# A two-layer convolution block on one core: steps of the next image enter at every second turn, and interpolation runs three pairs ahead

## The chip, the core and the metric

The kernel runs on one core of one Trainium2 chip. Its engines are TensorE (PE in the profile), VectorE (DVE), ScalarE (ACT), GpSimd (POOL) and SyncE (SP). Each takes its instructions in the order written for it, and they meet at semaphores only. The metric is the device time of one launch in microseconds (us), the median of several runs.

## What is computed

x has 8 images of 256 channels and 64x64 pixels, all in float32. Two layers follow each other, each added to its input:

```python
# layer 0: 3x3 local attention mixed with a generated 3x3 kernel
qkv = einsum('oc,bchw->bohw', w_qkv, gn(x))
attn = softmax(einsum('bhdl,bhdkl->bhkl', q, patches(k)))     # 4 heads, 9 taps
kern = einsum('hkc,bhcl->bhkl', w_kg, cat) + b_kg
x = x + w_proj @ (alpha * sum(kern * patches(v)) + beta * sum(attn * patches(v)))
# layer 1: modulated deformable 3x3 convolution of gn(x)
om = conv3x3(gn(x), w_off) + b_off          # 18 offsets, 9 masks for each pixel
v = bilinear sample of gn(x) at pixel + tap + offset, times sigmoid(mask)
x = x + einsum('bckhw,ock->bohw', v, w)
```

gn is a group normalisation over 32 groups.

## The kernel before, in words

An image is cut into 8 chunks of 512 pixels. Its work has two halves.

**The front** of an image is all of layer 0 and the preparation of layer 1. For each chunk: `xn` (ScalarE normalises x), `qkv.0` to `qkv.7` (TensorE; ScalarE evacuates each), `s` (four score steps, each two heads; after each, VectorE multiplies with a band mask, `banded`, L1303), `ext` (TensorE sums the scores to logits), `lg.out` (ScalarE), `lt` (TensorE transposes the logits), `soft.max`, `soft.exp`, `soft.mix` (VectorE and ScalarE), `soft.turn`, `soft.out` (TensorE, ScalarE), `sel` (four steps that spread the weights, each again with two band masks on VectorE), `pv` (two steps), `proj` (two steps) and `proj.end` (VectorE adds to x and takes statistics). Then `n.*` (the second normalisation), and for each chunk `pd` (ScalarE), `tp` and `om` (transposes for the table of pixels in DRAM, and the offset convolution) and `ot`, `w.pos`, `w.exp`, `w.mix` (indices and weights of the samples, mostly VectorE).

**The convolution** of an image runs over 72 units (8 chunks of 9 taps), each of two *pairs*, so m = 0 to 143. For each pair:

- `gather`: GpSimd issues two indirect DMAs (L883) that bring the four neighbours of 128 pixels each into a buffer of G (10 buffers, so 5 pairs). It waits until the interpolation five pairs before has freed it.
- `scale`: ScalarE multiplies the first neighbour by its weight (L1269). Where the offset phase of the front is running, VectorE does it (L1540).
- `lerp`: VectorE's interpolation, six operations (L1553, L1566) from G into V (6 buffers, so 3 pairs). It waits for the transposes of three pairs before.
- `turn`: TensorE first runs one contraction (`contract`, L902, four instructions of 512 columns) of an earlier unit and then transposes the pair (L1122). ScalarE copies the result to VT (L1283). After the first chunk a turn also holds `add_residual` (L1343) on VectorE, at two turns of each chunk: VectorE waits for the last contraction of the chunk before, TensorE's first contraction of the next chunk waits for that.

The convolution of image b runs together with the front of image b+1. `order_of_steps` writes one list for all engines, and every engine walks this list and picks its own parts. Generators yield the front's steps; `alternate` takes one step from each of several generators in turn, and `("idle",)` is an empty step that keeps dependent steps apart (`hop`). `fill(n, done)` takes steps until their weights (WEIGHT, at least 4 each) reach the share due at half-turn n. The banks of PSUM (six beside the two of the contraction) are handed out in the order of the list (`rotations`); TensorE waits until the last user has freed one. In the loop over m, the list before has:

```python
steps.append(("lerp", b, m))
done = fill(2 * m + 1, done)
steps.append(("turn", b, m - 1))
if m > 0:
    steps.append(("gather", b, 2 * (m - 1) + NG, 2 * m + NG))
scale(m + 2)
done = fill(2 * m + 2, done)
```

`s`, `ext`, `sel`, `pv` and `om` use a part of the TensorE array at a time (tiles of 64x128, 128x32, 32x128, 128x64); all other steps use it whole, 128x128. The first image's front runs before any convolution. The last image (`late`) has no front beside it: its convolution runs with the offset steps of its own chunks, and at every second pair ScalarE and VectorE work in halves that TensorE adds (`in_halves`, L1118, L1119, L1558).

Of the kernel before, what the change touches and what calls it, by code (L numbers as in the profile page):

```python
# [18 lines left out]
NCH = L // CH  # L19
# [5 lines left out]
NG = 10  # L25
# [6 lines left out]
PAIRS = 2 * UNITS  # L32
# [5 lines left out]
PROJ = 2  # L38
ADD = 2
HOP = 3  # L40
NEXT = 1
CHAIN = 5
COLLECT, TURN = 3, 2
NFIRST, NCONST = 9, 8
NST, ST = 6, 4
LATE_LEAD, LATE_PACE = 110, 440


# [36 lines left out]
    return late(b, NB) and m % 2 == 1  # L85


def offsets_fill(b, c, NB):


    return c + NCH if late(b, NB) else c


def alternate(*streams):
    streams = list(streams)
    while streams:
        for g in list(streams):
            step = next(g, "end")
            if step == "end":
                streams.remove(g)  # L100
            else:
                yield step


def together(*steps):
# [5 lines left out]
    return [t for s in steps for t in (s[1] if s[0] == "together" else (s,))]  # L111


def order_of_steps(NB):

    IDLE = ("idle",)
    have_kv, have_logits, have_x1 = set(), set(), set()
    offsets_run = [False]  # L120

    def hop(n):
        for _ in range(n):
            yield IDLE

    def norm(j, b):

# [25 lines left out]
    def scores(b, c):  # L153
        for par in (ODD, EVEN):
            while par == EVEN and c + 1 < NCH and (b, c + 1) not in have_kv:
                yield IDLE
            if b == 0:
                yield together(*(("s", b, c, par, hp) for hp in range(2)))
            else:
                for hp in range(2):  # L160
                    yield ("s", b, c, par, hp)
        yield from hop(COLLECT)
        yield ("ext", b, c)
        have_logits.add((b, c))
        yield ("lg.out", b, c)
        yield from hop(TURN)
        yield ("lt", b, c)

    def soften(b, c):


        if c == 0:
            yield from hop(CHAIN)
        for kind in ("soft.max", "soft.exp", "soft.mix", "soft.turn", "soft.out"):
            yield (kind, b, c)
            yield from hop(CHAIN if kind == "soft.mix" and c in (0, NCH - 2) else HOP if kind == "soft.mix" and c == NCH - 1 else 0)

    def last_scores(b, c):

# [4 lines left out]
    def mix(b, c):  # L184
        alone = 0 if c < NCH - 1 else HOP if b == 0 else NEXT
        if c < NCH - 1:
            yield from soften(b, c)
        else:
            yield from hop(2)
        while c > 0 and (b, c - 1) not in have_x1:  # L190
            yield IDLE
        for hp in range(2):

            while hp == 1 and c + 1 < NCH and (b, c + 1) not in have_logits:
                yield IDLE
            if b == 0:
                yield together(*(("sel", b, c, of, hp) for of in (OWN, BORDER)))
                continue
            for of in (OWN, BORDER):
                yield ("sel", b, c, of, hp)  # L200

                yield from hop(NEXT if c == NCH - 1 else 0)
        if b == 0:
            yield from hop(2 + alone)
            yield together(*(("pv", b, c, hp) for hp in range(2)))
            return
        for hp in range(2):
            yield from hop(1 + alone)
            yield ("pv", b, c, hp)

    def project(b, c):
        for _ in range(PROJ):
            yield IDLE
        for oh in range(2):
            yield ("proj", b, c, oh)
            for _ in range(ADD - 1):
                yield IDLE
        have_x1.add((b, c))
        yield ("proj.end", b, c)
# [59 lines left out]
            yield ("load_x", b + 1, c - 1)  # L279

    def weights(b, c):
        yield IDLE
        yield ("ot", b, c)
        yield ("w.pos", b, c)
        yield ("w.exp", b, c)
        yield ("w.mix", b, c)
# [9 lines left out]
    def offset_phase(b):  # L296

        before = iter(())
        yield ("pd", b, 0)
        yield from hop(HOP if b == 0 else NEXT)  # L300
        if late(b, NB):
            yield from table_phase(b)
            yield from offsets(b, 0)
            yield from weights(b, 0)
            return
        for c in range(NCH):
            yield from alternate(offsets(b, c), before)
            before = weights(b, c)
        yield from alternate(before, first_scores(b + 1) if b + 1 < NB else iter(()))
# [9 lines left out]
    def front(b):  # L319
        offsets_run[0] = False  # L320
        yield from layer0(b)
        offsets_run[0] = True
        yield from offset_phase(b)
        offsets_run[0] = False

    steps = list(begin())
# [2 lines left out]

    sets = (have_kv, have_logits, have_x1)  # L330
    before = [set(v) for v in sets]
    total = sum(weigh(s) for s in front(1))
    for v, old in zip(sets, before):
        v.clear()
        v.update(old)
    for b in range(NB):
        fr = front(b + 1) if b + 1 < NB else late_offsets(b)
        lead, pace = (LEAD, total) if b + 1 < NB else (LATE_LEAD, LATE_PACE)
        done = 0

        def fill(n, done):
            step = 0
            while done < lead + n * pace // (4 * UNITS) and step < BURST * pace // (4 * UNITS):
                s = next(fr, None)
                if s is None:
                    break
                steps.append(s)
                step += weigh(s)
                done += weigh(s)
            return done  # L350

        def scale(m):
            if m < PAIRS:
                steps.append(("scale", b, m, not offsets_run[0]))

        steps.append(("gather", b, 0, NG))
        scale(0)
        scale(1)
        done = fill(0, done)
        for m in range(PAIRS):  # L360
            steps.append(("lerp", b, m))
            done = fill(2 * m + 1, done)
            steps.append(("turn", b, m - 1))
            if m > 0:
                steps.append(("gather", b, 2 * (m - 1) + NG, 2 * m + NG))
            scale(m + 2)
            done = fill(2 * m + 2, done)
        steps.append(("turn", b, PAIRS - 1))
        steps.append(("conv.end", b))
        steps.extend(fr)  # L370
    return singly(steps)


# [153 lines left out]
def build(nc, x, wqk, wv, wn, wkx, bkg, alpha, beta, wproj, woff, boff, wconv,  # L527
          ident, g8, selx, selp, band, selo, base, out):
    NB = x.shape[0]
    steps = order_of_steps(NB)  # L530
# [3 lines left out]
    with ctx:  # L534
# [752 lines left out]
        def _(e):  # L1287
# [57 lines left out]
            for s in steps:  # L1345
# [222 lines left out]
                elif kind == "turn" and s[2] >= 0:  # L1568
                    b, m = s[1:]
                    u, pair = divmod(m, 2)  # L1570
                    c, t = unit(u)
                    if t == 1 and pair == 0 and u > 8:
                        add_residual(b * NCH + c - 1, 0)
                    elif t == 1 and pair == 1 and u > 8:
                        add_residual(b * NCH + c - 1, 1)
                elif kind == "conv.end":
                    for oh in range(2):
                        add_residual((s[1] + 1) * NCH - 1, oh)
# [73 lines left out]
```

## Time and profile before

| | us |
|---|---|
| median of 3 runs (5186.94 to 5206.48) | 5197.19 |
| the profiled execution | 5200.59 |
| its span | 5198.8 |
| PE busy | 4855.1 (93%) |
| DVE busy | 4324.4 (83%) |
| ACT busy | 2332.2 (45%) |
| POOL busy | 2257.9 (43%) |

The mean granted TensorE clock was 0.983 of full speed. The span goes from the first instruction to the last. A busy time counts every moment in which an engine has an instruction at work; idle time before an instruction is put down to what released it. Matmuls are pipelined, so a group's start to the next group's start says more of its cost than its length.

### The profile page before, as it was taken

To read this page: it belongs to the slowest core of one execution; us is meant where nothing else is said; L and a number is where in the kernel's file an instruction comes from. 1 tells how busy PE (TensorE), PEld (TensorE's weight loads), DVE (VectorE), ACT (ScalarE), POOL (GpSimd) and SP (SyncE) were. 2 spreads that over 40 slices of the span, in tenths; PEclk is the share of its full clock that TensorE was granted. 3 is DMA by queue.
4 is the path that set the end of the run, shared out by engine and by line. 5 is a ranking of instruction groups with operands and counts; after the bars stand their busy time and mean duration, and the time that the engine had idled before them with its cause. 6 is when DMAs were issued, how large, how long until landed. Compare 5 with 4: busy or idle time off the path is not lost. (4 is left out here: it accounts for less than half of the span.)

```text
span 5198.8 us, 80271 instructions
## 1 busy us (share of the span) xinstructions
PE 4855.1 (93%) x26864; PEld 2671.2 (51%) x26864; DVE 4324.4 (83%) x11040; ACT 2332.2 (45%) x5584; POOL 2257.9 (43%) x2311
## 2 busy tenths in 40 slices
PE   7889999999999999999999999999999999988888
PEld 4545554555545555455545555455554555544444
DVE  6848888888888888888889888888888888987776
ACT  2244444344453444444444444434444344455555
POOL 0014444444444444444444444444444444455565
PEclk9999999999999999999999999999999999999999
DMA  5447878878787878978789787888878878798888
GB/s 180 143 153 263 284 260 321 284 270 278 274 325 269 275 272 281 339 252 282 266 274 339 261 278 266 288 315 270 281 267 310 290 263 275 258 356 313 328 324 305
DMA packets 490804, 1446.79 MB, mean 278 GB/s; under 512 B 47380, under 2 KB 117404, under 8 KB 490140
## 3 DMA queue, kind: packets, MB, share of 16 engines
q0 software_dynamic: 331776, 1208.11, 66.9%
q1 hardware_dynamic: 158620, 233.55, 12.6%
q8 instruction: 219, 3.59, 0.3%
q14 instruction: 189, 1.55, 0.1%
HBM read 1309.08 MB, written 132.39 MB: 277 GB/s over the span
## 5 line engine op out<-in xcount | busy, mean ns | idle before, releaser
L883 POOL DMA_INDIRECT G<-table,IDX x2304 | 2257.0, 980 | 2902.3 <-DVE V L1566 2094.9
L902 PE MATMUL ps<-VT,s_wconv 128*128 128x512 f32 x4608 | 2273.9, 617 | 102.0 <-ACT VT L1283 37.7
L1566 DVE SCALAR_TENSOR_TENSOR V<-G,WT,V 128x256 f32<-128x256 f32 x4320 | 1892.7, 479 | 115.8 <-DVE V L1566 3.7
L1283 ACT ACTIVATE VT<-ps 128x512 f32<-128x512 f32 x1152 | 686.7, 596 | 2294.5 <-PE ps L1122 1848.3
L902 PEld LDWEIGHTS ps<-VT,s_wconv 128*128 128x128 f32 x4608 | 823.7, 193 | 919.1 <-issue 847.0
L1553 DVE SCALAR_TENSOR_TENSOR V<-G,WT 128x256 f32<-128x256 f32 x2304 | 1009.0, 478 | 244.6 <-ACT G L1269 135.4
L1122 PEld LDWEIGHTS ps<-s_ident,V 128*128 128x128 f32 x4320 | 539.1, 142 | 650.4 <-issue 647.1
L1303 DVE TENSOR_TENSOR E<-ps,s_band 128x512 f32<-128x512 f32 x1024 | 648.7, 682 | 268.9 <-PE ps L964 137.3
L1269 ACT ACTIVATE G<-G,WT 128x256 f32<-128x256 f32 x1872 | 846.4, 498 | 16.1 <-DMA G<-table,IDX 12.3
L1122 PE MATMUL ps<-s_ident,V 128*128 128x128 f32 x4320 | 655.5, 275 | 47.6 <-DVE V L1566 43.0
L940 PE MATMUL ps<-XN,s_wqk 128*128 128x512 f32 x1024 | 488.5, 605 | 19.7 <-ACT XN L1182 16.7
L964 PE MATMUL ps<-QB,KP 64*128 64x256 f32 (+2 forms) x2944 | 298.8, 340 | 2.0 <-DVE E L1303 1.3
L943 PE MATMUL ps<-s_wv,XN 128*128 128x292 f32 x1024 | 293.9, 416 | 0.0
L964 PEld LDWEIGHTS ps<-QB,KP 64*128 64x128 f32 x2944 | 235.8, 188 | 80.2 <-issue 62.6
L940 PEld LDWEIGHTS ps<-XN,s_wqk 128*128 128x128 f32 x1024 | 179.7, 191 | 183.5 <-issue 158.2
L1032 PE MATMUL ps<-E,VP 128*64 128x64 f32 (+2 forms) x3008 | 248.6, 318 | 8.2 <-DVE E L1303 8.2
L1080 PE MATMUL ps<-KP,s_woff 128*32 128x512 f32 x2048 | 244.2, 600 | 0.3 <-issue 0.3
L1045 PE MATMUL ps<-ACX,s_wproj 128*128 128x512 f32 x512 | 243.0, 598 | 1.4 <-ACT ACX L1139 1.4
L943 PEld LDWEIGHTS ps<-s_wv,XN 128*128 128x128 f32 x1024 | 180.0, 190 | 57.5 <-issue 20.1
L1032 PEld LDWEIGHTS ps<-E,VP 128*64 128x64 f32 x3008 | 171.8, 140 | 69.3 <-issue 21.1
L1233 ACT ACTIVATE KP<-X,gn 128x64 f32<-128x64 f32 (+1 forms) x396 | 192.8, 576 | 0.0
L1139 ACT ACTIVATE ACX<-ps 128x168 f32<-128x168 f32 (+1 forms) x384 | 112.3, 402 | 164.9 <-PE ps L1032 131.8
(109 smaller groups left out, 3008.4 us busy)
## 6 DMA issues: line engine op xcount, KB each, us to landing
table<-E SPq DMA_DIRECT2D x256, 256.0 KB
G<-table,IDX POOLq DMA_INDIRECT x2304
X<-in_x SPq DMA_DIRECT2D x64, 512.0 KB
G<-in_x SPq DMA_DIRECT2D x56, 512.0 KB, 4.3
x<-X SPq DMA_DIRECT2D x56, 512.0 KB, 5.5
R<-x SPq DMA_DIRECT2D x56, 512.0 KB
out<-R SPq DMA_DIRECT2D x56, 512.0 KB
out<-X SPq DMA_DIRECT2D x8, 512.0 KB
```

Of the source, the lines that this page charges most:

```text
L883: e.indirect_dma_start(G[a % NG][:, :], None, T[b % 2], bass.IndirectOffsetOnAxis(ap=IDX[:, col:col + 1], axis=0)).then_inc(d_g[a % NG], 16)
L902: mm = e.matmul(CV[oh][:, :], s_wconv[:, h, t, oh * P:(oh + 1) * P], VT[U % 2][:, h, :], start=(t == 0 and h == 0), stop=(t == 8 and h == 1))
L940: mm = e.matmul(bank[:, :], s_wqk[:, h, n * P:(n + 1) * P], XN[:, h, :], start=(h == 0), stop=(h == 1))
L943: mm = e.matmul(bank[:, 0:C + 36], XN[:, h, (n - 4) * P:(n - 3) * P], s_wv[:, h, :], start=(h == 0), stop=(h == 1))
L964: mm = e.matmul(to, k_view(g + t // 4)[part, hp, P * (t % 4):P * (t % 4) + P], QB[g % 2][part, hp, W * lo:W * hi], start=True, stop=True)
L1032: mm = e.matmul(BK[banks.place[use]][64 * (h % 2):64 * (h % 2) + 64, W * lo:W * hi], VP[:, (4 * g + t) % NVT, 64 * h:64 * h + 64], E[prods ...
L1122: mm = e.transpose(to, upper, s_ident[:, :])
L1269: e.activation(G[a % NG][:, 0:C], G[a % NG][:, 0:C], ACT.Copy, scale=WT[:, col, 0:1]).then_inc(act_scale, 1)
L1283: e.activation(VT[U % 2][:, :, 2 * P * pair:2 * P * (pair + 1)], BK[banks.place[use]][:, :].rearrange("p (h n) -> p h n", h=2), ACT.Copy). ...
L1303: e.tensor_tensor(two_rows(E[prods.place[use[0], use[1], use[3]]][:, :], *to), two_rows(BK[banks.place[use]][:, :], 0, 4, 2), band, ALU.mu ...
L1553: e.scalar_tensor_tensor(vt[:, :], gt[:, C:2 * C], WT[:, col, 1:2], gt[:, 0:C], ALU.mult, ALU.add).then_inc(lerp[0], 1)
L1566: e.scalar_tensor_tensor(vt[:, :], gt[:, q * C:(q + 1) * C], WT[:, col, q:q + 1], vt[:, :], ALU.mult, ALU.add).then_inc(lerp[q - 1], 1)
```

## The change

Three things are done to the list of steps. The convolution's own steps are reordered: `lerp` of pair m+2 and `scale` of pair m+4 stand around `turn` of pair m (before, `lerp` m+1 and `scale` m+3 did). The front's steps enter at odd m only, two fills together. And inside a front a dependent step waits for a gap (the stretch between two such entries) with `HELD` steps that don't count as progress, at most two steps with band masks enter in one gap, and in each entry `whole_first` moves `lt` and `qkv` ahead of tiled steps. `add_residual` moves with its contraction. Fronts written before `spread[0]` is set (the first image's) keep their `hop`s.

```diff
+GAP = 28
+def opened(m):
+    return m % 2 == 1
+IDLE, HELD = ("idle",), ("held",)
 def alternate(*streams):
     streams = list(streams)
     while streams:
+        moved = False
         for g in list(streams):
             step = next(g, "end")
             if step == "end":
                 streams.remove(g)
-            else:
+            elif step != HELD:
+                moved = True
                 yield step
+        if streams and not moved:
+            yield HELD
+def whole_first(part):
+    TILED, WHOLE = ("s", "ext", "sel", "pv", "om"), ("n.mean", "n.var", "qkv", "lt", "soft.turn", "proj", "tp", "ot")
+    part = list(part)
+    for i, s in enumerate(part):
+        if s[0] == "lt" or (s[0] == "qkv" and s[3] > 0):
+            to = i
+            for k in range(i - 1, -1, -1):
+                if part[k][0] in TILED:
+                    to = k
+                elif part[k][0] in WHOLE:
+                    break
+            if to < i and any(t[0] in TILED for t in part[i + 1:]):
+                part.insert(to, part.pop(i))
+    return part
...
+    def apart(n, first):
+        if not spread[0]:
+            yield from hop(first)
+            return
+        until = gaps[0] + n
+        while gaps[0] < until:
+            yield HELD
+    masked = [0, 0]
+    def masks(*step):
+        while spread[0] and masked[0] == gaps[0] and masked[1] == 2:
+            yield HELD
+        masked[:] = (gaps[0], masked[1] + 1 if masked[0] == gaps[0] else 1)
+        yield step
...
-                    yield ("s", b, c, par, hp)
-        yield from hop(COLLECT)
+                    yield from masks("s", b, c, par, hp)
+        yield from apart(1, COLLECT)
         yield ("ext", b, c)
         have_logits.add((b, c))
         yield ("lg.out", b, c)
-        yield from hop(TURN)
+        yield from apart(1, TURN)
         yield ("lt", b, c)
...
             yield (kind, b, c)
-            yield from hop(CHAIN if kind == "soft.mix" and c in (0, NCH - 2) else HOP if kind == "soft.mix" and c == NCH - 1 else 0)
+            if kind in ("soft.mix", "soft.out"):
+                yield from apart(1, 0 if kind == "soft.out" else CHAIN if c in (0, NCH - 2) else HOP if c == NCH - 1 else 0)
...
-                yield ("sel", b, c, of, hp)
-
-                yield from hop(NEXT if c == NCH - 1 else 0)
+                yield from masks("sel", b, c, of, hp)
...
+        yield from apart(1, 1 + alone)
         for hp in range(2):
-            yield from hop(1 + alone)
             yield ("pv", b, c, hp)
     def project(b, c):
-        for _ in range(PROJ):
-            yield IDLE
+        yield from apart(1, PROJ)
...
     def weights(b, c):
-        yield IDLE
+        yield from apart(1, 1)
...
         yield ("pd", b, 0)
-        yield from hop(HOP if b == 0 else NEXT)
+        yield from apart(1, HOP if b == 0 else NEXT)
...
-    total = sum(weigh(s) for s in front(1))
+    spread[0] = True
+    total = 0
+    for s in front(1):
+        total += weigh(s)
+        gaps[0] = total // GAP
...
                 if s is None:
                     break
-                steps.append(s)
+                if s == HELD and len(part) > 0 and part[-1] == HELD:
+                    break
+                part.append(s)
                 step += weigh(s)
                 done += weigh(s)
+            steps.extend(whole_first(part))
...
         done = fill(0, done)
+        interpolate(0)
+        scale(2)
+        interpolate(1)
+        scale(3)
         for m in range(PAIRS):
-            steps.append(("lerp", b, m))
-            done = fill(2 * m + 1, done)
-            steps.append(("turn", b, m - 1))
-            if m > 0:
-                steps.append(("gather", b, 2 * (m - 1) + NG, 2 * m + NG))
-            scale(m + 2)
-            done = fill(2 * m + 2, done)
-        steps.append(("turn", b, PAIRS - 1))
+            interpolate(m + 2)
+            if opened(m):
+                done = fill(2 * m + 1, done)
+                done = fill(2 * m + 2, done)
+                gaps[0] += 1
+            steps.append(("turn", b, m))
+            steps.append(("gather", b, 2 * m + NG, 2 * m + 2 + NG))
+            scale(m + 4)
         steps.append(("conv.end", b))
-        steps.extend(fr)
+        for s in fr:
+            gaps[0] += s == HELD
+            steps.append(s)
...
-                    if t == 1 and pair == 0 and u > 8:
+                    if t == 0 and pair == 1 and u > 8:
                         add_residual(b * NCH + c - 1, 0)
-                    elif t == 1 and pair == 1 and u > 8:
+                    elif t == 1 and pair == 0 and u > 8:
                         add_residual(b * NCH + c - 1, 1)
```

## Rows read from the trace of the kernel before

**Rows 1.** The page, part 1: the span, busy time and share of each engine.

```profile
span 5198.8 us, 80271 instructions
PE 4855.1 (93%) x26864; PEld 2671.2 (51%) x26864; DVE 4324.4 (83%) x11040; ACT 2332.2 (45%) x5584; POOL 2257.9 (43%) x2311
```

**Rows 2.** Windows by convolution: length, engine busy (count), granted clock, DMA share, GB/s.

```profile
2271.26:2895.73 624.47, 596.89 (x3320) 326.56 (x3318) 539.79 (x1391) 274.88 (x662) 281.27 (x289) 0.99 0.82 284
...
4155.94:4742.82 586.88, 538.84 (x2841) 292.08 (x2840) 498.00 (x1188) 284.24 (x670) 284.15 (x291) 0.98 0.83 291
4742.82:5198.80 455.98, 391.24 (x1654) 212.66 (x1652) 319.25 (x836) 258.50 (x587) 264.67 (x266) 0.94 0.87 317
```

**Rows 3.** Waits of PE in 2271.26 to 2895.73: who, total us, times, longest.

```profile
PE ps L1122 <- DVE V L1566: 5.1, 8, 1.9
PE ps L902 <- DVE R L1343: 4.8, 2, 2.5
PE ps L989 <- ACT LS L1139: 4.6, 2, 3.1
PE ps L1013 <- DVE E L1303: 2.8, 2, 1.5
PE ps L1013 <- ACT ACX L1134: 2.5, 1, 2.5
PE ps L940 <- ACT XN L1182: 2.2, 3, 1.2
```

**Rows 4.** PE's timeline, 2000 to 2020: start, length, line, count, [idle before].

```profile
2001.29 0.60 PE L1122 MATMUL ps<-s_ident,V 128*128 128x128 f32 x4
2001.73 1.88 PE L902 MATMUL ps<-VT,s_wconv 128*128 128x512 f32 x4
2003.61 0.63 PE L1122 MATMUL ps<-s_ident,V 128*128 128x128 f32 x4
2004.17 2.42 PE L979 MATMUL ps<-E,s_selx 128*32 128x176 f32 x48
2006.53 1.98 PE L902 MATMUL ps<-VT,s_wconv 128*128 128x512 f32 x4
...
2011.71 0.41 PE L1013 MATMUL ps<-ACX,s_selp 32*128 32x176 bf16 x6 [2.54 <-ACT ACX L1134]
2012.05 3.67 PE L902 MATMUL ps<-VT,s_wconv 128*128 128x512 f32 x4
```

**Rows 5.** A short window at that wait, columns as in Rows 2.

```profile
2010.70:2014.10 3.40, 2.39 (x9) 1.21 (x10) 3.21 (x8) 0.95 (x5) 2.50 (x3) 0.70 0.99 391
```

**Rows 6.** PE's timeline, 2234 to 2246, a wait and the group behind it.

```profile
2237.83 1.95 PE L979 MATMUL ps<-E,s_selx 128*32 128x176 f32 x48 [1.46 <-DVE E L1303]
2239.71 1.99 PE L902 MATMUL ps<-VT,s_wconv 128*128 128x512 f32 x4
```

**Rows 7.** The page's groups of VectorE's masks and of ScalarE's normalisation.

```profile
L1303 DVE TENSOR_TENSOR E<-ps,s_band 128x512 f32<-128x512 f32 x1024 | 648.7, 682 | 268.9 <-PE ps L964 137.3 <-PE ps L1013 70.3 <-issue 35.0
...
L1182 ACT ACTIVATE XN<-X,gn 128x512 f32<-128x512 f32 x114 | 85.7, 801 | 0.5 <-DVE gn L1404 0.5
```

**Rows 8.** DVE's timeline, 2267 to 2280, at the start of a convolution.

```profile
2269.48 0.30 DVE L1424 TENSOR_REDUCE sm<-ps 128x16 f32<-128x144 f32 x1
...
2271.23 0.87 DVE L1553 SCALAR_TENSOR_TENSOR V<-G,WT 128x256 f32<-128x256 f32 x2
2272.02 1.85 DVE L1566 SCALAR_TENSOR_TENSOR V<-G,WT,V 128x256 f32<-128x256 f32 x4
2273.79 0.30 DVE L1432 TENSOR_REDUCE sm<-SC 128x16 f32<-128x144 f32 x1
...
2276.42 0.87 DVE L1553 SCALAR_TENSOR_TENSOR V<-G,WT 128x256 f32<-128x256 f32 x2
```

**Rows 9.** Waits of PE, then of ACT, in the last convolution, 4742.82 to 5198.80.

```profile
PE ps L902 <- ACT VT L1283: 36.7, 8, 7.3
...
ACT VT L1283 <- remote: 99.7, 29, 6.6
```

More of the change, by code:

```diff
@@ L111, in singly @@
     return [t for s in steps for t in (s[1] if s[0] == "together" else (s,))]
+def whole_first(part):
[12 more added lines that the diff above has]
+    return part
 def order_of_steps(NB):
-    IDLE = ("idle",)
     have_kv, have_logits, have_x1 = set(), set(), set()
     offsets_run = [False]
+    gaps = [0]
+    spread = [False]
     def hop(n):
@@ L342, in fill @@
             step = 0
+            part = []
             while done < lead + n * pace // (4 * UNITS) and step < BURST * pace // (4 * UNITS):
@@ L354, in scale, with interpolate @@
                 steps.append(("scale", b, m, not offsets_run[0]))
+        def interpolate(m):
+            if m < PAIRS:
+                steps.append(("lerp", b, m))
         steps.append(("gather", b, 0, NG))
```

## Prediction, written before the changed kernel ran

> **What bounds the kernel now.** I read the page's busy shares first, then windows by convolution, then the waits of TensorE, then its timeline. TensorE is busy 4855 of 5199 us, VectorE 4324, ScalarE and GpSimd under half [rows 1]. A convolution with the next image's front beside it takes 624.5 us; TensorE is busy 596.9 of it, VectorE 539.8, and the DMA share is 0.82 [rows 2]. So TensorE sets the time, and what can be won there is its idle time, 624.47 - 596.89 = 27.6 us an image (4.4%), and what hides inside its busy time. The waits say what the idle time is: transposes that wait for the interpolation (5.1 us), contractions that wait for the residual (4.8), and front steps that wait for a step of their own chain on VectorE or ScalarE (4.6 for `lt`, 2.8 and 2.5 for `sel`, 2.2 for `qkv.0`) [rows 3]; the six make 22.0, and the remaining 5.6 are smaller ones of the same kinds.
>
> Two costs lie inside the busy time. The first is the change between the whole array and a tiled step. From the start of four transposes to the next contraction it is 2001.73 - 2001.29 = 0.44 us, to a tiled step 2004.17 - 2003.61 = 0.56; a contraction group takes 1.88 behind whole work and 1.98 behind tiled work [rows 4]. That is 0.12 + 0.10 = 0.22 us for each block of tiled steps. The second is the clock: behind the wait of 2.54 us the contraction took 3.67 us instead of 1.88 [rows 4], and the granted clock in that stretch was 0.70 [rows 5], so part of it ran at 1.2 GHz and not at 2.4. Behind a wait of 1.46 us the next contraction took 1.99 [rows 6]: no loss.
>
> By the Trainium skill (TensorE: Matmul & The Clock Gate, "A second HAM failure mode: psum-queue depth-cycling") frequent short idles between groups of matmuls alone can make the clock swing to half. Rows 6 speak against that here; what the rule would give is rival 2's price in every gap.
>
> **The change, part by part.** All is per image, of the six convolutions with a full front; a gap is two pairs, 624.5 / 72 = 8.7 us.
>
> (a) Switches. In the list before, the 112 tiled steps of an image (32 s, 32 sel, 8 ext, 16 pv, 24 om) stand in 91 blocks: a turn or a `qkv` is between most of them. After, they enter at 72 places instead of some 288, s and sel come in twos, both pv together, and `qkv` and `lt` are moved out from between them. I count 8 blocks for ext, 15 for s, 14 for sel, 8 for pv and some 9 for om: 54. 37 fewer at 0.22 is **-8 us** (bounds: 70 blocks, -5; 45, -10).
>
> (b) Waits that a gap removes. `ext` comes a gap after the masks, `lt` after the logits' copy, `sel` after `soft.out`, `pv` after its masks, `soft.turn` after `soft.mix`, `proj` after `pv`, `tp` after the first `pd`. A gap of 8.7 us covers what they wait for: ScalarE's copies, and masks of 4 x 0.68 = 2.7 us behind one interpolation [rows 7, 8]. So 4.6 + 2.8 + 2.5 and about 3 of the small ones go: **-13**.
>
> (c) The residual. TensorE's contraction for t = 0 comes two turns after the last contraction of the chunk before. VectorE's additions now stand at the same turns as those last contractions, one turn earlier than before. VectorE then waits where it would wait for a V buffer anyway. 4.8 goes: **-5**.
>
> (d) Interpolation three pairs ahead of its turn, not two. In mid-image this takes the last of the 5.1 us away, but those waits lie mostly at the start of an image, where VectorE works without a break: between 2269.5 and 2276.4 it does soft.max (1.75 us), a pair (2.56) and soft.mix (2.63) back to back [rows 8]. There the run-ahead has to be built up, before the first turn: VectorE does pairs 0 to 2 ahead of turn 0, and turn 0 comes right behind the first fill, not three fills later. I set **+3** (bounds: 0, since the last pair of the image before is also one earlier; one and a half pairs, +4). The same number of gathers and scales stand the same two pairs ahead of their interpolation, with the same 10 buffers of G, so GpSimd's queue sees nothing new; SP's steps keep their order among themselves.
>
> (e) Waits that the bunching adds. What isn't held back a gap now has no turn between its links: `xn` and `qkv.0`, `n.aggr` to `n.var`. TensorE begins the fill right after turn m-1. ScalarE has a copy and a scale first and then xn, 2 x 0.80 us [rows 7]. A wait of up to 2 us in each of 7 chunks, halved because it is often covered by steps ahead of it in the fill: +7 in place of 2.2, **+5**; the norm chain **+2** (bounds together: 0 and +16). Banks: two mask steps hold four of the six, but the turn's contraction, 1.9 us, stands before the transpose that needs one. Nothing. VectorE's own lateness costs nothing as long as TensorE has two pairs in hand: in a gap it needs 2 x 2.6 us for pairs and on average (539.8 - 72 x 2 x 2.6) / 72 = 2.3 for the rest, 7.5 of 8.7 [rows 2, 8].
>
> (f) Clock. Waits of over 2 us are two to three an image now [rows 3], each followed by a loss like 3.67 - 1.88 = 1.8 [rows 4]. One or two of them go: **-3** (bounds 0 and -5).
>
> Sum: -8 -13 -5 +3 +7 -3 = -19, of which -8 is idle time: 27.6 falls to about 20. I take **-20**.
>
> The seventh convolution (586.9 us, with the last image's shorter front) has 48 us idle [rows 2], part of it where VectorE alone sets the pace; I set -12. The last (456.0 us) has no front: 64.7 us idle, of which 36.7 are contractions that wait for ScalarE's copy, and ScalarE itself stood 99.7 us before such copies for a source the profile doesn't name [rows 2, 9]. Interpolating earlier doesn't help a late ScalarE; it shields the pairs behind it. I set -6 (bounds 0 and -20). What comes before the first contraction is planned without gaps and stay.
>
> 6 x -20 - 12 - 6 = -138. The profiled execution took 5200.6 us, 3.4 over the median of the runs; 5200.6 - 138 = 5062.6, against the median 5059. **Prediction 5058 us.**
>
> **The rivals.**
>
> 1. *The waits only move.* Bunching gives back all that the gaps win (the +16 of (e), +4 of (d), no clock gain) and the switches remain. Per image -5 -13 -5 +4 +16 = -3, at best -6: 5197 less 18 to 36 and at most 12 of the last two, 5150 to 5180. For it: TensorE starts each fill when VectorE has just been released by the same turn. Against: most links are held a gap apart.
>
> 2. *Slower: VectorE starves the turns.* V holds three pairs, so interpolation m+2 can't start before turn m-1 has been transposed, exactly when TensorE enters the fill. In a heavy gap VectorE has soft.max and soft.mix (1.75 + 2.63), four masks (2.7), `proj.end` (four operations of 512 columns, an estimate of 2.7 by the masks' 0.68) [rows 7, 8]: 9.8 us, and two pairs, 5.2: 15.0 against 8.7. It falls 6.3 us behind, against some 8 us in hand (two turns of 2.3 and a fill). It decides where two heavy gaps follow each other, or TensorE's wait grows past 2 us: then 3 us and the clock's 1.8 for each of 8 chunks, 38 an image against the 29 that (a), (b), (c) and (f) win: 9 an image, 5197 + 6 x 9 = 5250. For it: 4324 us of VectorE is not far below. Against: the mean gap needs 7.5.
>
> 3. *The plan doesn't fit.* A chunk's chain needs about 5.3 gaps by my count (masks four to a gap's two, soft, sel, pv), its steps by weight 6.6 gaps, and 72 are there. Should holds leave steps over, they run behind the convolution, with TensorE's work the same but each wait bare: 2.5 us as the longest ones now and the clock's 1.8 [rows 3, 4], 4.3 a gap; 4 gaps left give back 17 of the 20: 5160 to 5200.
>
> **How the numbers follow.** My forecast's own cases run from 4975 (the good bounds of (a), (d), (e), (f) make -33 an image, which with -20 and -20 for the last two is 4959; all at once is unlikely) to 5150 (only -7 an image). Chance 0.68. Rival 1: 0.14, of which 0.10 lies below 5171; rival 3: 0.05; rival 2: 0.13. The range 4975 to 5190 leaves out rival 2 and a little below. A measurement of this kernel can tell about 0.5%, 26 us, from no change: faster means below 5171, slower above 5223. Faster 0.78, same 0.09, slower 0.13.
>
> **What would show it.** An image's convolution of about 604 us with TensorE idle about 20; no waits of L902 for L1343, of L989 for L1139, of L979 for L1303; more of L940 for L1182; fewer groups of 1.98 us in the timeline; one low stretch of the clock fewer. The forecast is wrong if the wait of L1122 for L1566 grows past 10 us an image, if the image takes over 620 us, or if it falls below 593.

## The result and the profile after

The changed kernel takes 5292.46 us (5275.03 to 5294.59, 4 runs), the kernel before, measured beside it, 5193.37: a ratio of 1.018, 95% interval 1.015 to 1.021. The forecast was 5058, at best 4975 and at worst 5190; it went the other way. The profiled execution is the fastest of the four, 17 us under their median, which matters for the last convolution below.

The page's first part of the changed kernel, against [rows 1]:

```profile
span 5273.2 us, 80271 instructions
PE 4820.6 (91%) x26864; PEld 2709.8 (51%) x26864; DVE 4336.0 (82%) x11052; ACT 2346.9 (45%) x5572; POOL 2253.1 (43%) x2311
```

TensorE is busy 34.5 us less and the span is 74.4 us longer, so its idle time grew by 109 us. The granted clock fell from 0.983 to 0.975. The windows run from the last transposes of one convolution to the last transposes of the next, of the changed kernel and then of the one before:

```profile
2282.26:2917.25 634.99, 591.18 (x3320) 330.99 (x3319) 541.84 (x1393) 277.08 (x658) 279.77 (x288) 0.98 0.80 280
...
4200.79:4808.15 607.36, 540.47 (x2825) 303.58 (x2823) 504.83 (x1200) 284.97 (x669) 281.63 (x287) 0.96 0.80 280
4808.15:5263.93 455.78, 404.57 (x1778) 219.50 (x1777) 333.80 (x877) 277.21 (x624) 279.76 (x280) 0.97 0.91 335
```

```profile
2250.59:2875.06 624.47, 596.90 (x3321) 326.57 (x3319) 539.73 (x1391) 274.87 (x660) 281.27 (x288) 0.99 0.82 284
...
4125.10:4715.52 590.42, 541.71 (x2825) 296.11 (x2823) 503.44 (x1200) 282.62 (x669) 282.92 (x288) 0.98 0.83 290
4715.52:5189.53 474.01, 410.64 (x1778) 221.52 (x1777) 334.94 (x877) 274.68 (x624) 277.15 (x278) 0.94 0.87 319
```

A convolution beside a full front is 10.5 us longer here (the five that can be compared lost 10.5 to 16.8), though TensorE is busy 5.7 us less in it: its idle time went from 27.6 to 43.8. The one beside the last front lost 17 us. The last one, beside no front, is 18 us shorter in this pair of executions, but that can't be put down to the change. In two more profiles of the changed kernel (under the experiments) it took 479.5 and 474.9 us, and in one more of the kernel before 471.9, so the 18 us didn't come back. The losses of the others came back: 637 to 642 us beside a full front, 612 and 613 beside the last.

What TensorE waits for in that convolution of the changed kernel, and below it what VectorE waits for in the same stretch (who, total us, times, longest):

```profile
PE ps L1191 <- DVE E L1372: 6.6, 5, 2.1
PE ps L1069 <- DVE CB L1521: 5.8, 3, 2.5
PE ps L1009 <- ACT XN L1251: 5.6, 4, 2.3
PE ps L1082 <- DVE E L1372: 4.5, 5, 1.8
PE ps L1048 <- DVE E L1372: 4.0, 2, 2.0
PE ps L987 <- DVE mv L1447: 3.9, 1, 3.9
PE ps L1191 <- DVE V L1635: 2.1, 1, 2.1
PE ps L971 <- DVE R L1412: 2.1, 2, 1.2
```

```profile
DVE V L1622 <- PE ps L1191: 47.7, 13, 12.9
DVE R L1412 <- PE ps L971: 11.8, 3, 6.9
```

The lines moved by 67 to 69: L1191 are the transposes, L1009 `qkv`, L1048 `ext`, L1082 `sel`, L1372 the masks, L1622 the first operation of an interpolation. The waits for the residual and the logits' copy [rows 3] have gone or shrunk. In their place stand waits for VectorE's masks (L1372) and small sums (CB, mv). Two of the three rows for masks are waits for a bank: transposes and `sel` read nothing that a mask writes, they need a PSUM bank that a mask has still to read. Only `ext` waits for the masks' result. And VectorE, for whose work TensorE waits, has itself stood still 47.7 us ahead of interpolations until transposes freed a buffer of V; in the same stretch of the kernel before it was 1.5 us.

How the two go together shows in timelines, TensorE's and then VectorE's (start, length, line):

```profile
2442.31 0.41 PE L1082 MATMUL ps<-ACX,s_selp 32*128 32x176 bf16 x6
2443.05 1.20 PE L1033 MATMUL ps<-QB,KP 64*128 64x192 f32 x12 [0.34 <-DVE E L1372]
2444.18 1.98 PE L971 MATMUL ps<-VT,s_wconv 128*128 128x512 f32 x4
2446.00 0.60 PE L1191 MATMUL ps<-s_ident,V 128*128 128x128 f32 x4
2446.44 1.88 PE L971 MATMUL ps<-VT,s_wconv 128*128 128x512 f32 x4
2448.16 0.60 PE L1191 MATMUL ps<-s_ident,V 128*128 128x128 f32 x4
2450.76 1.95 PE L1048 MATMUL ps<-E,s_selx 128*32 128x176 f32 x48 [2.00 <-DVE E L1372]
```

```profile
2419.74 0.88 DVE L1622 SCALAR_TENSOR_TENSOR V<-G,WT 128x256 f32<-128x256 f32 x2 [4.29 <-PE ps L1191]
...
2428.01 0.88 DVE L1622 SCALAR_TENSOR_TENSOR V<-G,WT 128x256 f32<-128x256 f32 x2 [2.27 <-issue]
...
2440.43 2.47 DVE L1372 TENSOR_TENSOR E<-ps,s_band 128x512 f32<-128x512 f32 x4
2442.83 0.87 DVE L1622 SCALAR_TENSOR_TENSOR V<-G,WT 128x256 f32<-128x256 f32 x2
2443.62 1.85 DVE L1635 SCALAR_TENSOR_TENSOR V<-G,WT,V 128x256 f32<-128x256 f32 x4
2445.56 0.88 DVE L1622 SCALAR_TENSOR_TENSOR V<-G,WT 128x256 f32<-128x256 f32 x2
2446.36 1.86 DVE L1635 SCALAR_TENSOR_TENSOR V<-G,WT,V 128x256 f32<-128x256 f32 x4
2448.14 2.48 DVE L1372 TENSOR_TENSOR E<-ps,s_band 128x512 f32<-128x512 f32 x4
```

TensorE enters at 2442.31 and again at 2448.7: this gap is 6.4 us long, not 8.7, because an entry is filled by weights and this one holds one `sel`, one `s` and twelve idle steps. For VectorE the same gap is two pairs and four masks, 2442.83 to 2450.6, 7.8 us. The masks of the first entry, whose inputs TensorE computes from 2442.31 to 2444.2, are begun at 2448.1 behind both pairs, and `ext` waits 2.0 us. The two pairs could have waited in part: the first is transposed at 2448.16, the second only at 2455.03. And VectorE has no slack left here because it stood still before: 4.29 us at 2419.74 until the transposes freed a buffer of V, and 2.27 us at 2428.01, where the profile names no source but the transposes of three pairs before end at 2427.97. From there to 2450.6 it works without a break. That the time lost there is what the masks lack here is my reading of one place; the experiments test it.

### The profile page after: what moved, and what is told of

Read it like the earlier page. It is cut to its first block and busy times, and to the rows that moved or that the text cites. A ratio compares the mean times of both kernels' runs of the same rounds, so it can differ in the third digit from the quotient of the medians.

```text
span 5273.2 us, 80271 instructions
## 1 busy us (share of the span) xinstructions
PE 4820.6 (91%) x26864; PEld 2709.8 (51%) x26864; DVE 4336.0 (82%) x11052; ACT 2346.9 (45%) x5572; POOL 2253.1 (43%) x2311
## 5 line engine op out<-in xcount | busy, mean ns | idle before, releaser
L971 PE MATMUL ps<-VT,s_wconv 128*128 128x512 f32 x4608 | 2247.6, 611 | 77.6 <-issue 38.9
L1622 DVE SCALAR_TENSOR_TENSOR V<-G,WT 128x256 f32<-128x256 f32 x2304 | 1009.6, 479 | 506.5 <-PE ps L1191 348.0
L971 PEld LDWEIGHTS ps<-VT,s_wconv 128*128 128x128 f32 x4608 | 812.1, 194 | 780.5 <-issue 709.1
L1191 PEld LDWEIGHTS ps<-s_ident,V 128*128 128x128 f32 x4320 | 540.9, 142 | 667.3 <-issue 579.0
L1191 PE MATMUL ps<-s_ident,V 128*128 128x128 f32 x4320 | 656.3, 275 | 72.3 <-DVE E L1372 49.7
L1372 DVE TENSOR_TENSOR E<-ps,s_band 128x512 f32<-128x512 f32 x1024 | 639.2, 680 | 81.1 <-PE ps L1033 53.9
L1009 PE MATMUL ps<-XN,s_wqk 128*128 128x512 f32 x1024 | 488.9, 615 | 58.7 <-ACT XN L1251 39.4
L1009 PEld LDWEIGHTS ps<-XN,s_wqk 128*128 128x128 f32 x1024 | 190.9, 196 | 277.6 <-issue 209.1
L1012 PE MATMUL ps<-s_wv,XN 128*128 128x292 f32 x1024 | 277.1, 412 | 0.0
L1101 PEld LDWEIGHTS ps<-E,VP 128*64 128x64 f32 x3008 | 187.7, 142 | 60.2 <-issue 15.1
```

Of the source, the lines that this page charges most:

```text
L971: mm = e.matmul(CV[oh][:, :], s_wconv[:, h, t, oh * P:(oh + 1) * P], VT[U % 2][:, h, :], start=(t == 0 and h == 0), stop=(t == 8 and h == 1))
L1009: mm = e.matmul(bank[:, :], s_wqk[:, h, n * P:(n + 1) * P], XN[:, h, :], start=(h == 0), stop=(h == 1))
L1012: mm = e.matmul(bank[:, 0:C + 36], XN[:, h, (n - 4) * P:(n - 3) * P], s_wv[:, h, :], start=(h == 0), stop=(h == 1))
L1101: mm = e.matmul(BK[banks.place[use]][64 * (h % 2):64 * (h % 2) + 64, W * lo:W * hi], VP[:, (4 * g + t) % NVT, 64 * h:64 * h + 64], E[prods ...
L1191: mm = e.transpose(to, upper, s_ident[:, :])
L1372: e.tensor_tensor(two_rows(E[prods.place[use[0], use[1], use[3]]][:, :], *to), two_rows(BK[banks.place[use]][:, :], 0, 4, 2), band, ALU.mu ...
```

## The experiments

The runs fell on two kinds of chip. The kernel before took 5193 to 5220 us (the slower) or 5064 to 5065 (the faster), so ratios are compared within one kind only. All ratios are to the kernel before, measured beside the variant on the same chip, with 95% intervals. The changed kernel itself ran on the slower kind only. Times of single convolutions below are from the end of one's last contraction to the end of the next one's.

**The ruler**, both kernels unchanged, on the slower chip.

> The changed kernel, unchanged, beside the same kernel before as the experiments. By theory A it is above both variants that take VectorE's wait out of the fill's way (1.005 of before each): 1.015 to 1.025. If it is at 1.005 too, theory A is wrong and the difference to the variants was the chip's.

> The changed kernel once more, so that it stands on one chip with its variants: the kernel before took 5065 us in one call and 5193 to 5220 in the two others, so ratios are to be compared within a call. Ratio 1.015 to 1.025 whichever chip this is. Both theories say the same of it; it is the ruler.

Measured 1.0166 (1.0132 to 1.0201) and 1.016 (1.0138 to 1.0183).

> The kernel before, unchanged, for a profile on the chip of the other runs of this call. If this chip is the one of the last runs (before at 5065 and not 5193), its trace says where 128 us between two chips lie: either in waits for gathers (theory of slow transfers: scales on ScalarE that wait for a gather, and the last convolution) or in TensorE's granted clock.

Its profile came from the slower chip again (span 5201.9), so it didn't tell the two chips apart. A later pair did: the same kernel (residual alone, below) ran on both. These are waits of ScalarE there, on the faster and then on the slower:

```profile
ACT G L1269 <- DMA G<-table,IDX: 65.3, 122, 1.8
```

```profile
ACT VT L1283 <- issue: 172.3, 100, 5.5
ACT VT L1283 <- remote: 130.6, 39, 7.8
...
ACT LS L1139 <- remote: 55.2, 10, 6.4
ACT ACX L1139 <- remote: 42.9, 12, 5.9
```

On the slower chip ScalarE stands up to 7.8 us before its copies for a source that the profile doesn't name; on the faster one it has no such wait. A scale stands ahead of such a copy and waits for its gather, so late gathers are my reading; it is argued, not shown. The last convolution, where nothing runs beside it, shows the same difference plainest, faster and then slower (columns as in [rows 2]):

```profile
4650.00:5047.40 397.40, 389.56 (x1776) 210.57 (x1773) 336.11 (x878) 276.69 (x614) 279.26 (x278) 1.00 0.97 379
```

```profile
4757.00:5236.40 479.40, 414.43 (x1776) 221.91 (x1774) 334.92 (x877) 269.96 (x614) 276.91 (x278) 0.93 0.86 314
```

The same instructions take 82 us longer, of 189 in the whole run; TensorE is idle 65.0 us instead of 7.8 and its granted clock is 0.93 instead of 1.00. Every profile has 397 to 408 us here on the faster kind and 456 to 487 on the slower, whatever the variant.

**The order on VectorE alone.**

```diff
-            interpolate(m + 2)
             if opened(m):
                 ...
                 gaps[0] += 1
+            interpolate(m + 2)
```

> The changed kernel with one move: at odd m the fill stands ahead of interpolation m+2 and not behind it. TensorE's and ScalarE's lists stay the same; only VectorE's order differs. Theory A (interpolating three pairs ahead fills all three pairs of V, so VectorE waits for the transposes of turn m-1 and then does a pair before it comes to the fill's masks and sums, and TensorE meets them late): the 47.7 us an image in which VectorE waits for L1191 no longer delay the fill, TensorE's waits for masks, the CB copies and mv (29 us an image in the changed kernel) fall to under 12, the time to 5130 to 5190. Theory B (entering two fills at once is what hurts, whoever stands first on VectorE): within 20 us of the changed kernel's 5290.

> The fill ahead of interpolation m+2, once more. Theory A (VectorE held up in a full V ahead of the fill's masks): at least 0.8% below the changed kernel of this call. Theory C (the gain of this variant was the chip's, whose gathers land sooner): within 0.3% of it.

Faster chip: 1.0055 (1.0038 to 1.0072). Slower, beside the ruler: 1.0039 (1.0026 to 1.0051), that is 1.2% under the changed kernel. Theory A had the size too large (5130 to 5190, or 0.988 to 0.999 of before), but its sign and its 0.8% hold, and theory C is out. TensorE's list was the same, step for step, so three quarters of the loss came from where the fill stands on VectorE. The waits of TensorE on the slower chip, over the whole run, changed kernel and this one:

```profile
PE ps L1191 <- DVE E L1372: 49.1, 37, 4.2
...
PE ps L1048 <- DVE E L1372: 43.3, 22, 2.4
...
PE ps L1082 <- DVE E L1372: 26.3, 26, 2.0
```

```profile
PE ps L1191 <- DVE E L1372: 24.4, 28, 1.3
...
PE ps L1048 <- DVE E L1372: 15.1, 8, 2.4
PE ps L1082 <- DVE E L1372: 14.4, 15, 2.0
```

118.7 us for masks became 53.9. The waits for CB (44.0 and 42.4) and mv (27.7 and 25.4) stayed, against the expectation. VectorE still waits 222.6 us for V (343.7 in the changed kernel), but at odd m it now does so behind the fill's work and not ahead of it.

**Two pairs ahead.** `interpolate(m + 1)` and `scale(m + 3)` around turn m, the rest as changed.

> The changed kernel with interpolation two pairs ahead of its turn as before (interpolation m+1 and scale m+3 around turn m); the entries at every second turn, the holds and whole_first stay. Theory A: V no longer fills up, VectorE's waits for the transposes mostly go, 5150 to 5220. Theory B: 5280 or above, since less of the run-ahead is left to cover a heavy entry; waits of the transposes for V would grow past 10 us an image.

> Interpolation two pairs ahead, once more. Theory A: at least 0.8% below the changed kernel of this call. Theory C: within 0.3% of it. Where it stands to the kernel before says what the rest of the change (entries at every second turn, holds, whole_first, residual) is worth: I expect 1.000 to 1.008.

Faster: 1.005 (1.0033 to 1.0067). Slower: 0.9989 (0.9974 to 1.0004), 1.7% under the changed kernel. The run-ahead is the whole loss there; the rest of the change, against the kernel before, is worth nothing that can be measured on the slower kind and costs 0.5% on the faster. Theory B's fear, transposes that wait for V, came to 45.5 us in all, not 10 an image.

So the forecast gain is missing here too, and the waits of TensorE over the whole run say why, kernel before and this one on the slower kind. The gap took away what it was meant to: `lt` for its logits 33.3 to 9.1, `sel` for ScalarE 17.8 to 0, the residual 35.4 to 0. But `soft.turn` now waits 43.2 us for `soft.mix` (CB; 2.0 before) though a gap lies between them, `qkv.0` 37.4 for `xn` (16.7), the norm chain 33.7 for mv and gnt (3.5), and transposes 32.4 for a bank that a mask holds (0). That is 77 us gone and 124 new.

**Three pairs ahead in the kernel before.** `lerp` m+1 ahead of turn m-1, `scale(m + 3)`.

> The kernel before with the run-ahead alone: interpolation m+1 ahead of turn m-1, scale one pair earlier, nothing else. Theory A: it is slower by itself, 5230 to 5290, with VectorE waiting for transposes (L1122) by tens of us an image, and more waits of TensorE for the masks. Theory B: run-ahead does no harm, 5170 to 5195, and the last convolution gains the 18 us that it gained in the changed kernel.

Faster: 1.0168 (1.0151 to 1.0185). The same 1.7%, without holds or double entries. VectorE waited 310.8 us for transposes (10.4 in the kernel before), and TensorE 68.8 us for the residual instead of 35.4 and 45.4 for the masks of `ext` instead of 25.1 (the profile of before is from the slower kind). The last convolution gained nothing: 406.3 us, beside 397.4 for the residual alone.

**Two pairs ahead with a V of four buffers**, so that V is as full as six are at three.

```diff
-NV = 6
+NV = 4
-                    if M > 2:
-                        e.wait_ge(*filled(("vt", M - 3)))
+                    if M > 1:
+                        e.wait_ge(*filled(("vt", M - 2)))
```

> The variant two pairs ahead with four V buffers and not six, so that two pairs ahead fill V just as three pairs ahead fill six. Theory A (a full V holds VectorE before the fill's masks): it loses what three pairs ahead lost, 1.010 to 1.020 of before, with VectorE's waits for the transposes (33.7 us in the variant with six) at 250 to 400 us. If something else of the run-ahead costs the time (the ramp at the start of an image, scales or gathers at other places), it stays within 0.3% of the variant with six, 0.996 to 1.003.

Faster: 1.0214 (1.0197 to 1.0231), against 1.005 with six. VectorE's wait for a free V, with six and with four buffers:

```profile
DVE V L1620 <- PE ps L1189: 34.7, 10, 6.0
```

```profile
DVE V L1620 <- PE ps L1189: 373.8, 120, 12.9
```

The loss came back with the full V and with nothing else of three pairs ahead. That is theory A. Transposes didn't starve (56.0 us of waits for V with six buffers, 56.3 with four); TensorE's waits for masks and their banks rose from 59.0 to 88.5. V with eight buffers at three pairs ahead, the converse, wasn't tried.

**Double entries.** First every turn, three pairs ahead:

> The changed kernel with steps entering at every turn (the two fills of each m), the gap still counted at odd m, the rest as in the change. Theory A: still slower than before, since interpolation m+2 stands ahead of each fill: 5230 to 5300. Theory B: at or below 5200, though the blocks of tiled steps rise again and with them some 8 us an image.

Faster: 1.0333 (1.0316 to 1.035), more than theory A had (5300 is 1.021 of before). Entries at every turn with two pairs ahead stand at 1.007 on the same kind of chip (without `whole_first`, below), so run-ahead costs 2.6% here instead of 1.7. My reading is that with a full V an interpolation now stands in the way of every entry, not of every second. Then the kernel before with both fills at odd m only, its hops kept:

> The kernel before with nothing but the entries at every second turn (both fills at odd m, ahead of turn m-1); hops, run-ahead and residual as before. If entering in pairs is what hurts (theory B): 1.01 or more, with TensorE's waits for the masks and XN doubled. By theory A alone: 0.995 to 1.005, blocks of tiled steps some 20 an image fewer.

Slower: 1.0695 (1.0661 to 1.0729); TensorE waited 88.5 us for the masks of `ext` and 80.1 for those of `pv`. Theory A missed (0.995 to 1.005), B has it: without holds the double entry costs 7%. A hop is counted in steps, and two fills in one entry can swallow it; that this is the reason isn't tested. (Its fills precede turn m-1 and not turn m, so it isn't the change's entry to the letter.) Then holds without double entries, two pairs ahead:

```diff
             interpolate(m + 1)
-            if opened(m):
-                done = fill(2 * m + 1, done)
-                done = fill(2 * m + 2, done)
-                gaps[0] += 1
+            done = fill(2 * m + 1, done)
+            done = fill(2 * m + 2, done)
+            gaps[0] += opened(m)
             steps.append(("turn", b, m))
```

> Entries at every turn and two pairs ahead as before, so of the change the holds of a gap, the two-mask limit, whole_first and the place of the residual are left. If entering at every second turn is a loss by itself (as the kernel before with that alone, 1.07), this is faster than two ahead: 0.985 to 1.0. If holds need the double entries (a link of the chain then stands right at a gap's edge), it is slower: 1.01 to 1.02.

> Holds, whole_first and the residual with entries at every turn, two pairs ahead, once more. If what it wins is on the slower chip only (where before loses time to late gathers in front of ScalarE's copies), 1.005 to 1.010 where before takes 5065 and 0.994 where it takes some 5215. If it is the order itself, 0.994 on both.

Slower, twice: 0.9938 (0.9914 to 0.9961) and 0.994 (0.9919 to 0.9962). This is faster than both kernels on the slower kind; it didn't come to run on the faster one, where its nearest relatives stand at 1.007 and 1.008 (below), so it may be no gain there. Against two pairs ahead with double entries, measured beside it (0.9989), the double entry costs 0.5%. Some 13 of these 31 us lie in the convolution beside the last front alone, 599.4 us against 586.7; beside a full front it is 624.5 to 627.2 against 621.0 to 625.1. The list has 70 blocks of tiled steps an image here and 55 there, so fewer blocks weren't what counted.

**What earns the 0.6%** stays open. `steps.extend(part)` in place of `whole_first(part)`, and the residual's two conditions alone in the kernel before:

> Entries at every turn, two pairs ahead, without whole_first. It saves switches at 0.22 us a block: with it 0.994; without it, by my price of a block and some ten blocks an image, 15 us more, 0.996 to 0.998. If it also gets lt and qkv started before VectorE and ScalarE need them, more: 1.0 or above.

> The kernel before with the additions of the residual at the turns of their contractions and nothing else. By term (c) of the prediction 5 us an image and 35 us in all: 0.993 to 0.996, and no wait of L902 for L1343. If VectorE, which now stands still until TensorE has finished the contraction, is late with the masks behind it: 0.998 to 1.005.

> The kernel before with the residual's place alone, once more: 0.998 where before takes 5065; where it takes some 5215, 0.993 to 0.997 by term (c), 35 us in all.

Without whole_first 1.007 (1.0053 to 1.0087), but on the faster chip, where its partner hasn't run: inconclusive. It has 77 blocks an image instead of 70, and seven blocks at 0.22 us in six images are 9 us, 0.2%; if that were all, holds alone would be slower than before on the faster kind. The residual alone: 0.9984 (0.9974 to 0.9993) on the faster, 1.0033 (1.0015 to 1.005) on the slower. It isn't the source of the gain. TensorE waits no more for the residual, but VectorE now stands 133 us at it (61.0 before), and on the slower chip, where both have a profile, TensorE waits longer elsewhere: for `xn` 31.5 instead of 16.7, in `sel` for a bank 32.3 instead of 23.7, for V 47.0 instead of 43.0.

**Bare links taken apart**, on two pairs ahead and on holds alone: `xn` of the next chunk right behind `qkv.end`, `apart(1, n)` behind n.aggr and n.dev.

> The variant two pairs ahead, with the links that its trace shows bare taken apart: xn of the next chunk right behind the last qkv evacuation of this one (TensorE waited 41.9 us for XN), and a gap behind n.aggr and n.dev (25.6 us for mv, 8.1 for gnt). Theory A': what is left of the loss are such in-entry links, each at its price: some 60 us less than the variant, ratio 0.990 to 0.998. Theory B': the waits move on to the next link, 1.003 or more.

> Entries at every turn, two pairs ahead (0.994 of before), and with it xn of the next chunk right behind this chunk's last evacuation and a gap behind n.aggr and n.dev. TensorE waits there 31.2 us for XN and 20.0 for mv: if they are a loss of their own, 0.985 to 0.990; if the waits move on to gathers and the next link, 0.992 to 0.998.

Slower: 1.013 (1.0091 to 1.017), where two pairs ahead alone has 0.9989. Faster, on holds alone: 1.008 (1.0064 to 1.0097), above both expected ranges, but without its partner on that kind of chip. The first pair can be compared. The wait for XN fell from 37.4 to 17.0 us and that for mv went, and others took their place: 68.3 us for V instead of 45.5, 28.5 instead of 10.6 for `pd` (KP), and ScalarE's unnamed waits before its copies to VT grew from 138.8 to 245.6. Theory B' holds: taken out in this way, these waits weren't a gain.

## Why the prediction was wrong

Two things failed, and they add up. Run-ahead into a full V costs some 85 us, where (d) had 18. And the 138 us that the rest was to win didn't come even with two pairs ahead. As far as the waits show, both go back to one step of the prediction: that VectorE's lateness costs nothing, because a mean gap needs 7.5 of its 8.7 us.

- **What bounds the kernel**: right. TensorE's idle time decided, and went up.
- **(a) switches**: right. The list has 55 blocks of tiled steps an image (54 forecast, 91 before), and TensorE's busy time fell by 5.7 us an image, of 8, though its clock fell.
- **(b) a gap covers a link, -13**: this step failed. I took the mean gap of 8.7 us, and set against it four masks behind one interpolation. The gap at 2442 is 6.4 us, and VectorE has two interpolations and four masks in it, 7.8 us. The waits of `lt` (4.6 us) and of `sel` for ScalarE (2.5) did go; those of `ext` and `sel` for VectorE rose from 1.7 and 2.8 to 4.0 and 4.5, and 5.8 for CB came new. The 2.8 us of `sel` were also misread: `sel` reads nothing of VectorE's, so this was a wait for a bank, which a gap behind `soft.out` doesn't take away.
- **Banks, "nothing", and "VectorE's own lateness costs nothing as long as TensorE has two pairs in hand"**: wrong, and the heart of it. TensorE has its two pairs in hand (2.1 us an image of waits for them) and waits for VectorE all the same, through masks and banks: 15.1 us an image. Transposes that wait for a mask to free a bank are the largest row, 6.6 us; the contraction of 1.9 us ahead of them doesn't cover a pair and four masks.
- **(c) the residual, -5**: measured 4.8 to 2.1, right in kind and half in size; by itself in the kernel before it moved the time by -0.2% and +0.3%.
- **(d) run-ahead, +3**: the term that cost most. I saw that interpolation m+2 can't start before turn m-1 is transposed, priced it in rival 2 only, and there at the wrong place: not transposes that starve (2.1 us an image), but everything that stands behind the interpolation on VectorE. A full V costs 1.6 to 1.7% of the time in three comparisons, some 85 us; +3 an image would have been 0.3%.
- **(e) bare links, +7**: XN 2.2 to 5.6, mv and gnt 4.8: +8, right in size. The one attempt to take them away lost time.
- **(f) clock, -3**: wrong in sign. The mean granted clock fell from 0.983 to 0.975.
- **The seventh convolution, -12**: measured +17, and 612.0 and 613.2 us in the other two profiles against 590.4 and 591.8 before. Why it loses most isn't tested.
- **The last convolution, -6 with a bound of -20**: -18 in the first profile, nothing in the two others (479.5 and 474.9 us against 474.0 and 471.9 before). The first agrees with the bound by luck.
- **Rival 2** (5250, full V, slower) named the full V and the sign, at a chance of 0.13, but another path to the loss; that its 5250 lies near is luck. The sentence that should have raised it was in the text: VectorE "waits where it would wait for a V buffer anyway" says that V will be full all the time. Of the signs named in the prediction, an image over 620 us came true, L1122 waiting over 10 us for L1566 didn't.

## What to carry to other kernels

A producer that shares its engine with other work shouldn't be put so far ahead that it fills its buffer: here it then stood still in the list, and what was behind it came late. When entries are laid out by a mixed weight, compare each engine's own time in each entry, not the mean. And a change to an order is to be tried against the engine's list that it alone changes: one swap on VectorE gave back 1.2 of 1.6%. A gain that shows in one stretch of one profile should be looked for in a second profile before it is explained: the 18 us of the last convolution weren't there.

## What was not expected of the hardware

The kernel before took 5064 to 5065 us on some chips and 5193 to 5220 on others, and the medians on one chip and on the next of its kind agree within 0.6%. The clearest differences are ScalarE's unnamed waits and the last convolution (both above), and a granted clock of 0.991 against 0.976 for the residual alone. Whether late gathers cause the idle time and the clock follows, or something else lies behind both, no run shows. An order's worth depends on the kind of chip: two pairs ahead stood at 1.005 and 0.9989.
